# Graph layer: two norms from two products of one sum, bias addition on GpSimd, softmax links moved

## The chip, the cores and the metric

The kernel runs on one core of a Trainium2 chip. A core has five engines with instruction streams of their own: TensorE (PE, matrix products into PSUM), VectorE (DVE), ScalarE (ACT), GpSimd (POOL, here the issuer of indirect gathers) and SyncE (SP, here the issuer of plain transfers). They meet only at semaphores. The metric is the time of one execution on the device in microseconds (us); less is better.

## What is computed

Four graph layers over 50,000 nodes and 25,000 edges with 128 features, each followed by a residual sum and a layer norm. The change is in the third, a graph attention layer with an inner norm of its own:

```python
def _L2_gnn_ref(x, edge_index, edge_attr, W_l, b_l, W_r, b_r, W_e, att, bias, ln_w, ln_b):
    ...
    x_l = (x @ W_l + b_l).reshape(n, H, C)
    x_r = (x @ W_r + b_r).reshape(n, H, C)
    x_j = x_l[src]
    m = jax.nn.leaky_relu(x_j + x_r[tgt] + e_emb, NEG_SLOPE)
    logits = jnp.einsum('ehc,hc->eh', m, att)
    ...                                   # softmax over the edges of one target
    out = jax.ops.segment_sum(alpha[..., None] * x_j, tgt, num_segments=n)
    out = out.reshape(n, H * C) + bias
    out = jax.nn.gelu(out, approximate=False)
    h = out + x
    mu = jnp.mean(h, axis=-1, keepdims=True)
    var = jnp.mean((h - mu) ** 2, axis=-1, keepdims=True)
    return (h - mu) * jax.lax.rsqrt(var + LN_EPS) * ln_w + ln_b
...
x = _layernorm(x + _L2_gnn_ref(x, edge_index, edge_weight1, ...), axis=-1)
x = _layernorm(x + _L3_gnn_ref(x, src, dst, L3_gnn_W), axis=-1)
```

So a row x, which a norm has already centred, goes through two norms: norm 1 of gelu(...) + x, scaled by ln_w and shifted by ln_b, and norm 2 of that plus x.

## The kernel before

The edges are sorted by target and cut into 49 tiles of 512. The layer (`layer2`) is one loop of steps c = 0 to 62, written out for each engine by hand; the order of the statements is the order on the engine. In step c edge tile c gets its logits; tile e0 = c - 11 is weighed with the finished softmax and its plain nodes are projected; e1 = c - 12 goes through gelu and norm 1, e2 = c - 13 is scaled and centred again, e3 = c - 14 goes through norm 2 and is stored. Each tile has three blocks of 512 rows there: two of plain nodes (psP, two PSUM banks) and one of edge targets (psU, one bank). Up to step 48 all of this runs in every step; in steps 49 to 62 only the node part is left.

The softmax runs over seven runs s of seven tiles. Its serial part, the "links", is a chain of small VectorE operations on 112 or fewer columns: in step 7s+8 `running_maximum`, `maximum_between_chunks` and `exponents`, in step 7s+9 `running_sum`, `sum_between_chunks` and `weights`. PE turns columns to rows and back between them. I call such a step a softmax step and every other an ordinary one.

Norm 1 before, for tile e1 and then e2: PE multiplies the gelu (features on partitions) by the centring matrix I - 1/128, which also turns it to rows (L1363, psP and psU, operand `turns`); VectorE adds x (L1713, L1717: `pre1`); ScalarE squares it (L1538), VectorE sums (L1586), ScalarE forms rstd (L1564); VectorE scales (L1582: `n`); PE turns the three blocks back (L1358, from `n`); ScalarE applies ln_w and ln_b (L1528, L1532, into `turns`); PE centres and turns to rows a second time (L1363); VectorE adds x (L1748, L1765: `pre2`). Norm 2: square (L1569), sum (L1586), rstd (L1524), and scaling to x3o (L1582) and x4o (half on L1582, half in four ScalarE copies, L1543). `pre2` is a single buffer: VectorE may refill it only when x3o and x4o of the tile before are made.

The logits of tile c come from z, zsl and zl on VectorE (L1754, L1758, L1761). At the end of a step PE turns the gathered rows of edge tile c+1 (`turn_edges`, L1358 from `xd_xs`) and projects the nodes of e0 (L1471, `y`); the next step begins with L1391. POOL issues eight gathers for a tile (L1292), two tiles ahead, each time after PE has turned a tile. `by_row`, `quarters` and `scaled` only cut 1536 columns in 128-column rows and multiply each by its factor.

## Time and profile before

| | |
|---|---|
| runs | 3518.30, 3537.49, 3529.63 us (median 3529.63) |
| the profiled execution | 3540.14 us |
| span of its trace | 3538.4 us |
| mean granted clock of TensorE, share of full | 0.878 |
| PE busy, of the span | 2701.9 us (76%) |
| DVE | 2616.7 us (74%) |
| ACT | 2012.3 us (57%) |
| POOL | 1863.6 us (53%) |

The profile gives, for one execution, when each engine worked and what released it when it had waited. A row of a timeline has the start and the duration; the next row of the same engine often starts some 0.08 us before the printed end, since operations overlap a little. The difference of two starts is therefore what an operation costs its engine, and the duration is what another engine waits for. The third layer runs from about 1896 to 2955 us of the span: steps 0 to 10 end near 2050 us, the tail without edges begins near 2745 us. The fourth layer takes the rest, 583 us.

### The profile page before, as it was taken

Reading aid. Unit: us, or ns where it says so; the run is one execution under the profiler, and the core shown is the slowest. Engines: PE = TensorE matmul, PEld = TensorE weight load, DVE = VectorE, ACT = ScalarE, POOL = GpSimd, SP = SyncE. Lnnn points to the kernel's source line nnn. Section 1 sums busy time; section 2 is a strip of 40 time slices with the busy share of each in tenths; the row PEclk is TensorE's granted clock in tenths of the full one; section 3 lists DMA queues with packets and bytes.
Section 4 is the critical chain, followed back from the end, with each engine's and each line's share of the span. In section 5 each row is a group of like instructions: output and inputs, shape, how many; then the busy total and the mean of one; then the engine's idle time right before and its main releaser. Section 6 shows DMA issues by size and latency. Waiting matters only on the chain. (4 is left out here: it accounts for less than half of the span.)

```text
span 3538.4 us, 46258 instructions
## 1 busy us (share of the span) xinstructions
PE 2701.9 (76%) x14325; PEld 1792.3 (51%) x14325; DVE 2616.7 (74%) x3171; ACT 2012.3 (57%) x3400; POOL 1863.6 (53%) x1771
## 2 busy tenths in 40 slices
PE   7799999689999778878785789999999774332332
PEld 3466666466666545555553246666666553221221
DVE  6589999889999868888884269999999994222322
ACT  0167777556665558878784258888888782111111
POOL 4477787333333276766663654554453003666665
PEclk6699999899999989999997899999999996566655
DMA  6357666556666556666662156666666653222221
GB/s 202 100 173 222 212 221 220 189 176 197 197 202 199 160 167 207 210 207 208 197 205 74 47 159 172 188 196 193 183 194 174 183 171 107 58 64 63 74 69 39
DMA packets 474800, 573.34 MB, mean 162 GB/s; under 512 B 65347, under 2 KB 283133, under 8 KB 474431
## 3 DMA queue, kind: packets, MB, share of 16 engines
q1 hardware_dynamic: 412744, 457.19, 42.0%
q0 software_dynamic: 56480, 111.88, 11.6%
q8 instruction: 119, 1.95, 0.2%
q10 hardware_dynamic: 5334, 1.32, 0.2%
q14 instruction: 123, 1.00, 0.1%
HBM read 353.51 MB, written 220.55 MB: 162 GB/s over the span
## 5 line engine op out<-in xcount | busy, mean ns | idle before, releaser
L1292 POOL DMA_INDIRECT g_xd_xs<-table_x,dst_row x196 | 211.8, 1081 | 360.4 <-PE g_psT L1358 250.7
L1804 POOL DMA_INDIRECT f_xs<-table_x,src_row x196 | 192.0, 980 | 312.5 <-POOLq L1216 253.1
L775 POOL DMA_INDIRECT c_xs<-table_x,src_row x196 | 185.5, 946 | 303.9 <-PE c_psT L916 250.6
L765 POOL DMA_INDIRECT c_xs<-table_h,src_row x196 | 206.9, 1056 | 193.0 <-PE c_psT L909 94.0
L1867 ACT ACTIVATE f_reluT<-f_psY 128x512 f32<-128x512 f32 x49 | 29.3, 597 | 472.6 <-DMA table_x<-g_x3o 329.2
L497 POOL DMA_INDIRECT xs<-in_x,src_i x196 | 224.7, 1147 | 101.6 <-issue 54.0
L482 POOL DMA_INDIRECT xd<-in_x,dst_i x196 | 222.9, 1137 | 96.3 <-issue 47.9
L1811 POOL DMA_INDIRECT out<-f_xo,end_i x196 | 198.7, 1014 | 121.1 <-DVE f_xo L1904 61.6
L1292 POOL DMA_INDIRECT g_xd_xs<-table_x,src_row x196 | 218.6, 1116 | 59.8 <-issue 59.8
L765 POOL DMA_INDIRECT c_xd<-table_h,dst_row x196 | 200.8, 1025 | 59.8 <-issue 59.8
L1363 PE MATMUL g_psP<-w_center,g_turns 128*128 128x128 f32 x1568 | 197.1, 279 | 13.6 <-ACT g_turns L1492 9.1
L1363 PEld LDWEIGHTS g_psP<-w_center,g_turns 128*128 128x128 f32 x1568 | 187.0, 194 | 32.5 <-ACT g_turns L1492 12.7
L1586 DVE TENSOR_REDUCE g_var<-g_sq 128x12 f32<-128x1536 f32 x98 | 171.7, 1752 | 37.8 <-ACT g_sq L1538 34.6
L1841 PE MATMUL f_psE<-w_center,f_reluT 128*128 128x128 f32 x392 | 79.8, 368 | 153.2 <-ACT f_reluT L1867 117.7
L1896 DVE SCALAR_TENSOR_TENSOR f_pre<-f_x3r,f_psE 128x512 f32<-128x512 f32 x49 | 33.5, 684 | 203.8 <-DMA out<-g_x4o 193.1
L1023 ACT ACTIVATE c_xo<-c_pre,c_rstd 128x128 f32<-128x128 f32 x588 | 182.4, 390 | 1.6
L1841 PEld LDWEIGHTS f_psE<-w_center,f_reluT 128*128 128x128 f32 x392 | 70.5, 270 | 165.0 <-ACT f_reluT L1867 124.6
L1846 PE MATMUL f_psY<-f_red,w_w3t 128*128 128x512 f32 x98 | 77.6, 885 | 99.7 <-issue 68.6
L1122 DVE TENSOR_TENSOR c_pre<-c_psE,c_x1r 128x512 f32<-128x512 f32 x147 | 98.6, 686 | 73.0 <-remote 55.2
L1913 DVE TENSOR_TENSOR_SCAN f_red<-f_cont,f_red,f_psT 128x512 f32<-128x512 uint8 x48 | 61.3, 1277 | 112.7 <-DMA g_packed<-logits 76.0
L1471 PE MATMUL g_psP<-g_nodeT,w_w_l 128*128 128x512 f32 x196 | 107.1, 673 | 45.7 <-DVE g_pre L1748 44.2
L1853 PE MATMUL f_psT<-w_ident,f_xs 128*128 128x128 f32 x196 | 45.2, 374 | 116.9 <-DMA f_xs<-table_x,src_row 111.1
(330 smaller groups left out, 8669.8 us busy)
## 6 DMA issues: line engine op xcount, KB each, us to landing
g_share<-shares SPq DMA_DIRECT2D x196, 192.0 KB
xn<-in_x SPq DMA_DIRECT2D x49, 512.0 KB
table_x<-xo SPq DMA_DIRECT2D x49, 512.0 KB
table_x1b<-xb SPq DMA_DIRECT2D x49, 512.0 KB
c_xn<-table_x SPq DMA_DIRECT2D x49, 512.0 KB
table_h<-c_xo SPq DMA_DIRECT2D x49, 512.0 KB
c_xn<-table_h SPq DMA_DIRECT2D x49, 512.0 KB
c_x1r<-table_x1b SPq DMA_DIRECT2D x49, 512.0 KB
```

The costliest lines, as they stand in the source:

```text
L482: pool.indirect_dma_start(out=quarters(h.xd0[:, s, :])[j], out_offset=None, in_=io["x0"], in_offset=edge_index(h.dst_i, n, j)).then_inc(h. ...
L497: pool.indirect_dma_start(out=quarters(h.xs0[:, s, :])[j], out_offset=None, in_=io["x0"], in_offset=edge_index(h.src_i, n, j)).then_inc(h. ...
L765: pool.indirect_dma_start(out=quarters(rows[:, s, :])[j], out_offset=None, in_=table, in_offset=edge_index(columns, now.n, j)).then_inc(la ...
L775: pool.indirect_dma_start(out=quarters(xs[:, s, :])[j], out_offset=None, in_=table, in_offset=edge_index(h.src_row, now.n, j)).then_inc(sr ...
L1023: ins = nc.scalar.activation(quarters(xo[:, g.slot, j // 4, :])[j % 4], quarters(pre[:, g.slot, j // 4, :])[j % 4], ACT.Copy, scale=rstd[: ...
L1292: pool.indirect_dma_start(out=quarters(xd_xs[:, s, k, :])[j], out_offset=None, in_=table, in_offset=edge_index(columns, now.n, j)).then_in ...
L1363: ins = nc.tensor.matmul(o, x, h.w["center"][:, :], start=True, stop=True)
L1471: ins = nc.tensor.matmul(psP[:, k, :], h.w["w_l"][:, :], nodeT[:, e0 % 2, k, :], start=True, stop=True)
L1586: nc.vector.tensor_reduce(var[:, :], by_row(sq[:, :, :].rearrange("p b n -> p (b n)")), AX_X, ALU.add).then_inc(ready, 1)
L1804: pool.indirect_dma_start(out=quarters(xs[:, s, :])[j], out_offset=None, in_=table, in_offset=edge_index(h.src_row, now.n, j)).then_inc(sr ...
L1811: pool.indirect_dma_start(out=io["out"], out_offset=edge_index(h.end_i, old.n, j), in_=quarters(xo[:, s, :])[j], in_offset=None, bounds_ch ...
L1841: ins = nc.tensor.matmul(o, x, h.w["center"][:, :], start=True, stop=True)
```

## The change

Since x is centred already, centring gelu + x equals centring gelu and adding x. The new kernel adds x before the product, with features on partitions (`gx`), and takes two products of that one sum: with the centring matrix C, for the squares of norm 1, and with C diag(ln_w) C, called `twice_centred`, for what norm 2 needs. Dividing by the deviation of norm 1 is done behind the second product, and C ln_b, as a row (`ln_b_row`), is added to x by GpSimd.

For each node tile, removed: twelve PE transposes of `n`, two ScalarE operations with ln_w and ln_b, the VectorE scaling of `n`, the VectorE half of x4o. Added: four PE transposes of the edge rows (`xe_turned`), four more ScalarE copies for x4o (eight in all), one GpSimd addition over 128x1536. The four residual additions on VectorE become two additions into `gx` (1024 and 512 columns), two scalings from PSUM (`scaled_n`, `scaled_e`) and one addition over 1536 columns. The square of norm 1 is read from PSUM in two parts; the squares of the two norms get buffers of their own. Moved: the square of norm 2 to the next step's start on ScalarE, the z products on PE ahead of the softmax's row products, and on VectorE the links behind x3o and behind the scaling. In the set-up two VectorE scalings, two PE products and two VectorE copies are new. The core of the diff:

```diff
+            nc.vector.tensor_scalar(centre_w[:, :], h.w["center"][:, :], h.col("ln_w"), None, ALU.mult).then_inc(norm_rows, 1)
+            nc.vector.tensor_scalar(spread_b[:, :], ones[:, :], h.col("ln_b"), None, ALU.mult).then_inc(norm_rows, 1)
...
+            nc.tensor.matmul(psm[:, P:2 * P], h.w["center"][:, :], centre_w[:, :], start=True, stop=True)
+            nc.tensor.matmul(psm[:, 2 * P:3 * P], spread_b[:, :], h.w["center"][:, :],
+                             start=True, stop=True).then_inc(norm_turned, 1)
...
+            for n in range(ends):
+                if is_tile(n):
+                    gather(n)
+                e = n - 2 - lag
+                if is_tile(e):
+                    pool.wait_ge(n_turned, e + 1)
+                    pool.wait_ge(xe_turned, e + 1)
+                    wait(pool, x3_ready, e - 1)
+                    x = by_row(rows[:, e % 4, :, :].rearrange("p b n -> p (b n)"))
+                    nc.gpsimd.tensor_tensor(x, x, bias, ALU.add).then_inc(biased, 1)
...
@@ block.tensor
                 if is_tile(e1):
-                    pe.wait_ge(gn_ready, e1 + 1)
+                    pe.wait_ge(x2e_landed[e1 % 4], 16 * (e1 // 4 + 1))
+                    wait(pe, scaled_e, e1 - 1)
+                    turned_rows(psU[:, 0, :], rows[:, e1 % 4, 2, :]).then_inc(xe_turned, 1)
+                    pe.wait_ge(gxn_ready, e1 + 1)
                     for k in range(2):
-                        ins = centred(psP[:, k, :], gn[:, k, :])
+                        ins = to_rows(psP[:, k, :], gx[:, e1 % 2, k, :], h.w["center"])
                     ins.then_inc(en_ready, 1)
...
                 if is_tile(e2):
-                    pe.wait_ge(n1_ready, e2 + 1)
-                    pe.wait_ge(n_kept, min(e0 + 1, STEPS))
+                    pe.wait_ge(sq1n_ready, min(e1 + 1, STEPS))
+                    wait(pe, scaled_n, e2)
                     for k in range(2):
-                        ins = turned_rows(psT[:, k, :], n1[:, k, :])
-                    ins.then_inc(n1n_turned, 1)
+                        ins = to_rows(psP[:, k, :], gx[:, e2 % 2, k, :], h.twice_centred)
+                    ins.then_inc(fn_ready, 1)
...
                     pe.wait_ge(n_kept, e0 + 1)
-                    wait(pe, pre1n_ready, e1 + 1)
-                    wait(pe, pre2n_ready, e2 + 1)
+                    wait(pe, sq1n_ready, e1 + 1)
+                    wait(pe, scaled_n, e2 + 1)
...
@@ block.scalar
-                    nc.scalar.activation(sq1[:, :, :], pre1[:, :, :], ACT.Square).then_inc(sq1_ready, 1)
+                    act.wait_ge(en_ready, e1 + 1)
+                    wait(act, var1_ready, e1)
+                    nc.scalar.activation(sq1[:, 0:2, :], psP[:, :, :], ACT.Square).then_inc(sq1n_ready, 1)
+                    act.wait_ge(ee_ready, e1 + 1)
+                    nc.scalar.activation(sq1[:, 2, :], psU[:, 0, :], ACT.Square).then_inc(sq1e_ready, 1)
...
-                    for j in range(4):
-                        ins = nc.scalar.activation(quarters(x4o[:, 0, :])[j], quarters(pre2[:, 0, :])[j], ACT.Copy,
-                                                   scale=rstd2[:, j:j + 1])
-                    ins.then_inc(x4a_ready, 1)
+                    for k in range(2):
+                        for j in range(4):
+                            ins = nc.scalar.activation(quarters(x4o[:, k, :])[j], quarters(pre2[:, k, :])[j], ACT.Copy,
+                                                       scale=rstd2[:, 4 * k + j:4 * k + j + 1])
+                    ins.then_inc(x4_ready, 1)
...
@@ block.vector
+                if is_tile(e2):
+                    wait(dve, x3_ready, e2)
+                    wait(dve, x4_ready, e2)
+                    wait(dve, sq2_ready, e2)
+                    dve.wait_ge(rstd1_ready, e2 + 1)
+                    dve.wait_ge(fn_ready, e2 + 1)
+                    scaled(pre2[:, 0:2, :], psP[:, :, :], rstd1[:, e2 % 2, 0:8], 2, scaled_n)
...
+                    scaled(pre2[:, 2:3, :], psU[:, :, :], rstd1[:, e2 % 2, 8:12], 1, scaled_e)
+                    dve.wait_ge(biased, e2 + 1)
+                    dve.wait_ge(scaled_n, e2 + 1)
+                    dve.wait_ge(scaled_e, e2 + 1)
+                    nc.vector.tensor_tensor(pre2[:, :, :], pre2[:, :, :], rows[:, e2 % 4, :, :],
+                                            ALU.add).then_inc(pre2_ready, 1)
```

PE in an ordinary step, before: from the turning of the node rows (`xn`) to the first product of the next step.

```order
L1358 MATMUL g_psT<-w_ident,g_xn 128x128 x8
L1363 MATMUL g_psP<-w_center,g_turns 128x128 x8
L1363 MATMUL g_psU<-w_center,g_turns 128x128 x4
L1358 MATMUL g_psT<-w_ident,g_n 128x128 x8
L1358 MATMUL g_psU<-w_ident,g_n 128x128 x4
L1439 MATMUL g_psZ<-g_edgeT,w_w_r 128x512
L1440 MATMUL g_psZ<-g_erow,w_e_row 128x512
L1442 MATMUL g_psZ<-g_edgeT,w_lr 128x512
L1363 MATMUL g_psP<-w_center,g_turns 128x128 x8
L1363 MATMUL g_psU<-w_center,g_turns 128x128 x4
L1358 MATMUL g_psT<-w_ident,g_xd_xs 128x128 x8
L1471 MATMUL g_psP<-g_nodeT,w_w_l 128x512 x2
```

The same stretch of PE after the change (`rows` holds the node and edge rows).

```order
L1372 MATMUL g_psT<-w_ident,g_rows 128x128 x8
L1372 MATMUL g_psU<-w_ident,g_rows 128x128 x4
L1377 MATMUL g_psP<-w_center,g_gx 128x128 x8
L1377 MATMUL g_psU<-w_center,g_gx 128x128 x4
L1437 MATMUL g_psZ<-g_edgeT,w_w_r 128x512
L1438 MATMUL g_psZ<-g_erow,w_e_row 128x512
L1440 MATMUL g_psZ<-g_edgeT,w_lr 128x512
L1377 MATMUL g_psP<-twice_centred,g_gx 128x128 x8
L1377 MATMUL g_psU<-twice_centred,g_gx 128x128 x4
L1372 MATMUL g_psT<-w_ident,g_xd_xs 128x128 x8
L1479 MATMUL g_psP<-g_nodeT,w_w_l 128x512 x2
```

The transposes of `n` are gone, and the four of the edge rows stand ahead of the first product.

VectorE around x3o in step 7s+8, before (`m_row`, `m_in` and `m_line` are the link between chunks).

```order
L1713 TENSOR_TENSOR g_pre<-g_psP,g_xn 128x1024
L1717 TENSOR_TENSOR g_pre<-g_psU,g_x2e 128x512
L1604 COPY g_m_row<-g_psA 1x4x32
L1607 SCALAR_TENSOR_TENSOR g_m_in<-g_reach_row,g_m_row 1x132
L1609 COPY g_m_line<-g_m_in 1x128
L1611 COPY g_m_row<-g_m_in 1x4
L1582 TENSOR_TENSOR g_x3o<-g_pre,g_rstd 128x1536
L1582 TENSOR_TENSOR g_x4o<-g_pre,g_rstd 128x512
L1586 TENSOR_REDUCE g_var<-g_sq 128x12
```

VectorE there after the change.

```order
L1600 SCALAR_TENSOR_TENSOR g_m_here<-g_far,g_top 128x112
L1583 TENSOR_TENSOR g_x3o<-g_pre,g_rstd 128x1536
L1605 COPY g_m_row<-g_psA 1x4x32
L1608 SCALAR_TENSOR_TENSOR g_m_in<-g_reach_row,g_m_row 1x132
L1610 COPY g_m_line<-g_m_in 1x128
L1612 COPY g_m_row<-g_m_in 1x4
L1587 TENSOR_REDUCE g_var<-g_sq 128x12
L1583 TENSOR_TENSOR g_pre<-g_psP,g_rstd 128x1024
L1617 COPY g_m<-g_psA 128x1
```

The link now stands behind x3o, and the scaling from PSUM ahead of the exponents.

POOL after the change; before, only the gathers stand there.

```order
L1298 DMA g_xd_xs<-table_x,src_row 128x128 x4
L1311 TENSOR_TENSOR g_rows<-g_rows,ln_b_row 128x1536
L1298 DMA g_xd_xs<-table_x,dst_row 128x128 x4
```

The addition for a tile stands between the gathers of two edge tiles.

## Rows read from the trace of the kernel before

**Rows 1.** Windows: stretch, us, busy PE, PEld, DVE, ACT, POOL, clock, DMA share, GB/s.
```profile
2160.00:2745.00 585.00, 551.73 (x3043) 363.01 (x3042) 539.27 (x586) 487.13 (x707) 276.68 (x239) 1.00 0.67 189
```
**Rows 2.** DVE in one ordinary step, timeline (start, duration, what, idle before).
```profile
2463.11 1.76 DVE L1582 TENSOR_TENSOR g_x3o<-g_pre,g_rstd 128x1536 f32<-128x1536 f32 x1 [0.84 <-ACT g_rstd L1524]
2464.79 0.68 DVE L1582 TENSOR_TENSOR g_x4o<-g_pre,g_rstd 128x512 f32<-128x512 f32 x1
2466.25 1.75 DVE L1586 TENSOR_REDUCE g_var<-g_sq 128x12 f32<-128x1536 f32 x1 [0.77 <-ACT g_sq L1538]
2467.92 1.22 DVE L1748 TENSOR_TENSOR g_pre<-g_psP,g_xn 128x1024 f32<-128x1024 f32 x1
2469.05 0.68 DVE L1754 TENSOR_TENSOR g_z<-g_psZ,g_values 128x512 f32<-128x512 f32 x1
...
2470.31 0.68 DVE L1761 SCALAR_TENSOR_TENSOR g_zl<-g_z 128x512 f32<-128x512 f32 x1
...
2476.84 1.28 DVE L1705 TENSOR_TENSOR_SCAN g_agg<-g_share,g_agg,g_values 128x512 f32<-128x512 f32 x1
```
**Rows 3.** PE in the same step, timeline.
```profile
2469.28 1.96 PE L1471 MATMUL g_psP<-g_nodeT,w_w_l 128*128 128x512 f32 x4 [0.17 <-DVE g_pre L1748]
2471.09 1.10 PE L1391 MATMUL g_psZ<-g_edgeT,w_w_l 128*128 128x512 f32 x2
...
2472.97 1.05 PE L1402 MATMUL g_psA<-g_zl,g_att_a 128*36 128x512 f32 x2
...
2474.81 1.09 PE L1358 MATMUL g_psT<-w_ident,g_xn 128*128 128x128 f32 x8
2475.74 1.95 PE L1363 MATMUL g_psP<-w_center,g_turns 128*128 128x128 f32 x16
```
**Rows 4.** ACT in the same step, timeline.
```profile
2461.04 1.28 ACT L1512 ACT_TABLE_LOAD   x1
2462.33 0.30 ACT L1516 ACTIVATE g_lnv<-g_var,eps 128x8 f32<-128x8 f32 x1
...
2462.99 1.19 ACT L1528 ACTIVATE g_turns<-g_psT,cols 128x1024 f32<-128x1024 f32 x1
...
2466.11 1.27 ACT L1543 ACTIVATE g_x4o<-g_pre,g_rstd 128x128 f32<-128x128 f32 x4
2467.28 0.68 ACT L1549 ACTIVATE g_low<-g_psZ,x2b_self 128x512 f32<-128x512 f32 x1
...
2476.10 1.01 ACT L1501 ACTIVATE g_nodeT<-g_psT 128x1024 f32<-128x1024 f32 x1
2477.00 1.11 ACT L1505 ACTIVATE g_values<-g_psZ,cols 128x1024 f32<-128x1024 f32 x1
2478.00 0.59 ACT L1510 ACTIVATE g_alike<-g_psA 36x512 f32<-36x512 f32 x1
```
**Rows 5.** POOL in the same step, timeline.
```profile
2469.89 0.95 POOL L1292 DMA_INDIRECT g_xd_xs<-table_x,dst_row  x1 [6.07 <-PE g_psT L1358]
...
2479.18 0.94 POOL L1292 DMA_INDIRECT g_xd_xs<-table_x,src_row  x1 [0.30 <-issue]
```
**Rows 6.** POOL in the set-up, view of groups by line and form.
```profile
L419 POOL IOTA i_rev_row<- 98x256 int32 x1 | 0.3, 337 | 0.0
```
**Rows 7.** DVE, timeline: z in steps 7s+8 and 7s+9, and the link.
```profile
2504.18 0.68 DVE L1754 TENSOR_TENSOR g_z<-g_psZ,g_values 128x512 f32<-128x512 f32 x1
...
2515.94 0.28 DVE L1604 COPY g_m_row<-g_psA 1x128 f32<-1x128 f32 x1
...
2517.24 1.76 DVE L1582 TENSOR_TENSOR g_x3o<-g_pre,g_rstd 128x1536 f32<-128x1536 f32 x1 [0.23 <-DVE g_m_row L1611]
...
2544.80 0.68 DVE L1754 TENSOR_TENSOR g_z<-g_psZ,g_values 128x512 f32<-128x512 f32 x1
```
**Rows 8.** DVE in the tail, timeline.
```profile
2877.93 1.20 DVE L1713 TENSOR_TENSOR g_pre<-g_psP,g_xn 128x1024 f32<-128x1024 f32 x1
...
2892.60 1.20 DVE L1713 TENSOR_TENSOR g_pre<-g_psP,g_xn 128x1024 f32<-128x1024 f32 x1
```

More of the change, by code:

```diff
@@ L341, in _ @@
             link(nc.vector.tensor_scalar(h.x2b_self[:, :], h.b_self[:, :], 0.2, None, ALU.mult))
+            dve.wait_ge(norm_turned, 1)
+            link(nc.vector.tensor_copy(h.twice_centred[:, :], psm[:, P:2 * P]))
+            link(nc.vector.tensor_copy(h.ln_b_row[:, :], psm[:, 2 * P:3 * P]))
             dve.wait_ge(rows_turned, 1)
@@ L1229, in layer2 @@
         edgeT, nodeT = sb("edgeT", [P, 2, 2, TILE]), sb("nodeT", [P, 2, 2, TILE])
[L1230 removed]
+        rows = sb("rows", [P, 4, 3, TILE])
         erow = sb("erow", [P, 2, TILE])
@@ L1283, in _, with gather @@
         def _(pool):
-            def step(t):
-                now = t.tile(0)
-                s = now.slot
-                wait(pool, src_landed[s], 64 * now.half)
-                wait(pool, dst_landed[s], 64 * now.half)
-                wait(pool, e_turned, now.n - 1)
+            def gather(n):
+                s = n % 2
+                wait(pool, src_landed[s], 64 * (n // 2))
+                wait(pool, dst_landed[s], 64 * (n // 2))
+                wait(pool, e_turned, n - 1)
                 for k, columns, landed in ((0, h.dst_row, dst_landed), (1, h.src_row, src_landed)):
@@ L1452, in _ @@
                                      start=True, stop=True).then_inc(d_cols, 1)
-                if is_tile(e2):
-                    pe.wait_ge(affn_ready, e2 + 1)
-                    pe.wait_ge(pre1n_ready, min(e1 + 1, STEPS))
-                    for k in range(2):
-                        ins = centred(psP[:, k, :], affT[:, k, :])
-                    ins.then_inc(fn_ready, 1)
-                    pe.wait_ge(affe_ready, e2 + 1)
-                    centred(psU[:, 0, :], affT[:, 2, :]).then_inc(fe_ready, 1)
                 if is_tile(c + 1):
@@ L1463, in _ @@
                     wait(pe, n_kept, e0 + 1)
-                    wait(pe, affn_ready, e2 + 1)
                     turn_edges(c + 1)
@@ L1931, in build @@
         h.w_edge_row, h.w_e_row = square("w_edge_row"), square("w_e_row")
+        h.twice_centred, h.ln_b_row = square("twice_centred"), square("ln_b_row")
         h.b_vs = sb("b_vs", [P, 2])
```

183 lines of the change are left out of this document (75 added, 108 removed).

## The prediction

> **What bounds the kernel now.** I read the windows first, then one step of the third layer on each engine. In the full steps of that layer, 585 us of the trace, PE is busy 551.7 us, VectorE 539.3 and ScalarE 487.1, at a clock of 1.00 [rows 1]. No engine is the only bound; what counts is how the engines' orders close from one step to the next. The reader is to see a step of 17.56 us: z starts at 2469.05 and, two ordinary steps on, at 2504.18 [rows 2, 7]. VectorE works 15.95 us of it and waits twice, 0.84 us for the factor of norm 2 and 0.77 us for the square of norm 1 [rows 2]; both come from ScalarE, which runs without a pause through its chain from nodeT to the x4o copies [rows 4]. POOL idles 6 us of a step [rows 5]. So a gain needs three things together: PE's 94%, VectorE's 91% and the ScalarE chain all have to shrink.
>
> **PE.** Eight transposes take 0.93 us of PE (2474.81 to 2475.74), eight centring products 1.79 [rows 3], whose rows count two passes a product (x16 against x8). Twelve transposes go (1.4 us), four come (0.5 us): 0.9 us less; the products with `twice_centred` are as many and of the same form as the second centring. PE needs some 15.8 us.
>
> **VectorE.** The half of x4o goes: 0.65 us (0.68 long) [rows 2]. The rest only changes places: scaling `n` and four additions were 1.69 + 1.12 + 0.60 + 1.13 + 0.60 = 5.1 us; now gx 1.13 + 0.60, scalings from PSUM 1.13 + 0.60, the 1536 addition 1.67 and 0.1 for the wait on the scaling just before it: 5.2 us. An operation of a form costs the same from PSUM as from SBUF (pre2 over 1024 columns 1.22 us) [rows 2]. VectorE needs 15.4 us.
>
> **ScalarE.** The two affine operations go (1.19 us the one [rows 4]), four copies of x4o come: four take 1.17 us (2466.11 to 2467.28), eight 2.34, and the last one ends 0.10 later [rows 4]. The square of norm 1 is cut in two and reads PSUM. PSUM forms of 1024 columns cost 0.90 (nodeT, 2476.10 to 2477.00) to about 1.1 us (affine); I take 0.95, and 0.60 for the 512 part, from `low` (0.68 long) [rows 4]. Two table loads per step stay. ScalarE needs 14.9 us.
>
> **The loop that now sets the step.** `pre2` is still one buffer, and y still waits until VectorE has emptied psP. So the cycle is: y, L1391 and L1392, the logits' two products, turning the node rows; on ScalarE nodeT, values, alike, table load, two logarithms, exponential, the two squares, eight copies; on VectorE the scaling; back to y. In order: 1.81 (2469.28 to 2471.09) + 1.88 (to 2472.97) + 1.84 (to 2474.81) + 1.09 + 0.03 = 6.65 on PE [rows 3]; 0.90 + 1.00 + 0.60 + 1.29 + 0.66 (2462.33 to 2462.99) + 0.95 + 0.60 + 2.44 = 8.44 on ScalarE [rows 4]; 0.03 + 1.22 + 0.14 = 1.39 for the scaling and the way back to PE [rows 2, 3] (0.14 is from the end of pre2 at 2469.14 to y). Together 16.48 us, above all three sums of work, so it closes last; 1.08 less than 17.56. Bounds: with PE alone bounding 15.8, with the squares at the price of the affine pair 16.8.
>
> What is moved hardly counts: the z products stand earlier on PE by what the transposes took; the square of norm 2 moves over a gap of ScalarE; SP issues the node rows behind one wait instead of two, a step and more ahead of their use. The four transposes of edge rows wait for psU of the last but one tile, long free.
>
> **GpSimd's addition.** No row shows GpSimd adding tensors. From below I take VectorE's 1.76 us for the same columns [rows 2]; GpSimd's own index row, 256 columns in 0.34 us [rows 6], is 1.3 ns a column and would make it 2.0, my value. From above I take the slowest elementwise form of the trace, the scan with 1.28 us for 512 columns [rows 2], 3.8 us. The gate holds the addition until x3o of the step is done. Behind it are queued the eight gathers of a tile, 10.2 us from first to last [rows 5]. From the end of x3o to the turning of those rows I count a step and 2.2 us, 18.7 us; less 10.2 to 11.2 for gathers, some 2 for the last landing and 0.8 for starting leaves about 5 us for the addition. Up to there it is hidden. VectorE asks for the result behind both scalings, 5 us after x3o: also hidden. So at 2.0 as at 3.8 us the term is nothing. If the cover is gone, the excess over 5 us falls on VectorE in every step. The Trainium skill (GPSIMD Engine Reference, Performance versus the Vector engine) gives 4497 ns for such an addition over 2048 columns; an estimate from that page for 1536 would be 3.4 us, and the sum would stay.
>
> **The sum.** From step 11 the full steps that are ordinary and settled number 24: 24 x 1.08 = 25.9 us. Softmax steps: both together take 40.62 us now (z at 2504.18 and 2544.80) [rows 7]. VectorE is full there, so the links are 40.62 - 2 x 15.95 = 8.7 of it; afterwards it needs 2 x 15.4 + 8.7 = 39.5 and some 0.1 of waits: 1.0 less, five pairs, 5 us. Tail: a step is 14.67 us (2877.93 to 2892.60) [rows 8], all VectorE; afterwards 15.4 less z, zsl and zl (1.86) plus 0.2 of waits is 13.7; eight steps, 8 us. The set-up adds six small operations, at most 1 us. In all 25.9 + 5 + 8 - 1 = 38 us. On the profiled execution's 3540.1 that is 3502; that execution lies 10.5 us above the median of the runs, so I predict 3529.6 - 38 = 3492 us.
>
> **Rival 1: the addition holds up VectorE's small operations (about the same as before).** In a softmax step the link now starts right where the addition does, behind x3o. It is four operations, 1.30 us before (2515.94 to 2517.24) [rows 7], among them a scan of two SBUF rows and SBUF copies. If VectorE and GpSimd cannot read SBUF at once, the link waits for the rest of the addition, and the step with it, since VectorE is full there. Twelve softmax steps have an addition. At 1.76 us an addition (VectorE's own row) the price is 12 x 1.5 = 18 us, result 3510; at 3.8 us 12 x 3.5 = 42, result 3534. In ordinary steps the gate puts the addition beside the reduction, the scaling from PSUM, z and zsl; the first operation with two SBUF operands, zl, comes 4.6 us behind x3o. For it: VectorE is without a pause at exactly this place, so that any delay counts in full. Against it: gathers run on POOL through half of each step and no row of VectorE is longer for it; but a gather is no addition of tensors. The first two of the four operations may also be through before the addition starts, some 0.8 us behind its release; then the price is smaller. The Trainium skill states it as a rule (SBUF — State Buffer, Who interferes with whom): a VectorE instruction with two SBUF inputs and a GpSimd instruction that reads SBUF exclude each other for a whole instruction. With the 3.4 us of the page on GpSimd it would cost 37 us and leave 3529.
>
> **Rival 2: slower.** Same mechanism, decided by the length of the addition with its start. Beyond 4.6 us zl waits in every step, and in the tail the 1536 addition. At 5 us with 0.8 for starting: 12 x 4.7 = 56 for the links, and 32 ordinary and tail steps x 1.2 = 38; 3492 + 94 = 3586. It outweighs the gain from about 3.5 us of length on. Without any exclusion the same side is reached only when the addition is over 5 us and holds the gathers back: at 8 us the turning comes 3 us late in every second step, 24 x 1.5 = 36 and more.
>
> **Rival 3: the step does not close at 16.5.** If squares from PSUM cost 1.19 + 0.77 or x4o's copies 0.35 us each, ScalarE's chain grows by 0.3 to 0.5 us, and if z or the values then fall behind PE, a step gains 0.4 us and not 1.1: 3492 + 24 x 0.7 = 3509.
>
> **How the numbers follow.** About 0.5%, 18 us, is what a measurement can tell from no change here. Forecast 3492, chance 0.50, own range 3476 to 3511. Rival 1: 0.27, 3510 to 3534, a fifth of it on the side of faster. Rival 3: 0.10, at the border. Rival 2: 0.13. Faster: 0.48 + 0.05 + 0.04 = 0.57; same: 0.02 + 0.22 + 0.06 = 0.30; slower 0.13. The range leaves out rival 2 and a little below: 3474 to 3538.
>
> **What would show it.** In the trace after: ordinary steps from z to z of 16.5 us; ahead of the scaling (1024 columns) VectorE idle for about 0.5 us, released by x4o on ScalarE; x3o to the next reduction without idle time in ordinary steps. Rival 1 shows as idle time of 1 to 3.5 us in front of `m_in` or `m_line`, and only there; rival 2 as idle time in front of zl or the 1536 addition, or of PE in front of the turning of edges. POOL's new row gives the length that decides. Wrong at the root would be a step whose last wait is neither x4o nor GpSimd.

## The result: slower by 0.7%

| | before | after |
|---|---|---|
| median of 6 runs each, taken together | 3520.78 us (3518.30 to 3537.49) | 3550.61 us (3535.71 to 3561.02) |
| ratio after / before | | 1.0066, interval 1.0045 to 1.0088 |
| the profiled execution | 3540.14 us | 3549.30 us |
| its span | 3538.4 us | 3547.5 us |
| third layer, first z to last x3o | 1027.3 us | 1039.1 us |

The change makes the kernel slower by about 0.7%. The whole difference of the spans, 9 us, lies in the third layer, which is 11.8 us longer. The forecast was 3492, with a range up to 3538; the time lies outside it.

The window over the full steps, after (stretch, us, busy PE, PEld, DVE, ACT, POOL, clock, DMA share, GB/s), to be read against [rows 1]:

```profile
2160.00:2745.00 585.00, 532.14 (x2705) 334.42 (x2705) 532.62 (x539) 453.19 (x778) 413.08 (x271) 0.94 0.65 185
```

POOL went from 277 to 413 us. PE, VectorE and ScalarE are less busy than before, in part because the change gives them less to do in a step. But the steps did not get shorter by as much, and the clock of PE, 1.00 before, is 0.94. I then looked at the distance from z to z, step by step:

| | before | after | predicted |
|---|---|---|---|
| ordinary step | 17.56 | 16.40, some 17.3 to 17.5 | 16.48 |
| pair of softmax steps (mean of five) | 40.7 | 46.7 (22.9 + 23.8) | 39.6 |
| step behind the pair | 17.56 | 18.5 to 18.8 | 16.48 |
| tail, ordinary (x3o to x3o) | 14.66 to 14.92 | 13.56 | 13.7 |
| tail, last softmax step | 16.72 | 20.16 | not worked out by itself |

VectorE in an ordinary step, after (timeline: start, duration, what, idle before), against [rows 2]:

```profile
2465.89 1.27 DVE L1705 TENSOR_TENSOR_SCAN g_agg<-g_share,g_agg,g_values 128x512 f32<-128x512 f32 x1
2467.70 1.76 DVE L1583 TENSOR_TENSOR g_x3o<-g_pre,g_rstd 128x1536 f32<-128x1536 f32 x1 [0.54 <-issue]
2469.37 1.74 DVE L1587 TENSOR_REDUCE g_var<-g_sq 128x12 f32<-128x1536 f32 x1
2471.48 1.23 DVE L1583 TENSOR_TENSOR g_pre<-g_psP,g_rstd 128x1024 f32<-128x1024 f32 x1 [0.36 <-ACT g_x4o L1549]
...
2473.88 0.68 DVE L1754 SCALAR_TENSOR_TENSOR g_zl<-g_z 128x512 f32<-128x512 f32 x1
```

The scaling waits for x4o as foretold, 0.36 us. zl, two SBUF operands, is undisturbed at 0.68.

VectorE in a softmax step, where the link stands behind x3o, against [rows 7]; then POOL over the same time:

```profile
2518.13 1.73 DVE L1583 TENSOR_TENSOR g_x3o<-g_pre,g_rstd 128x1536 f32<-128x1536 f32 x1
2519.78 0.27 DVE L1605 COPY g_m_row<-g_psA 1x128 f32<-1x128 f32 x1
2520.09 4.34 DVE L1608 TENSOR_TENSOR_SCAN g_m_in<-g_reach_row,g_m_row 1x132 f32<-1x132 f32 x1
2524.46 0.21 DVE L1610 COPY g_m_line<-g_m_in 1x128 f32<-1x128 f32 x1
```

```profile
2518.37 2.31 POOL L1298 DMA_INDIRECT g_xd_xs<-table_x,src_row  x1 [0.30 <-issue]
2520.70 3.44 POOL L1311 TENSOR_TENSOR g_rows<-g_rows,ln_b_row 128x1536 f32<-128x1536 f32 x1
2524.29 0.96 POOL L1298 DMA_INDIRECT g_xd_xs<-table_x,dst_row  x1 [0.16 <-issue]
```

The scan over 132 elements of one partition, 0.42 us before, is printed with 4.34 us. It ends at 2524.43, the addition at 2524.14; in all twelve softmax steps that have an addition the link's scan ends 0.28 to 0.30 us behind the addition's end. `m_in` took 3.66 to 4.35 us in six of the seven softmax runs and 0.42 in the first, which has no addition beside it; `d_in`, the link of the second softmax step, 3.53 to 3.54 in six of seven. VectorE shows no idle time in front of it. What takes an operand from PSUM is not longer: of the layer's rows beside an addition (behind 2100 us), 35 scalings over 1024 columns, 35 reductions and 25 rows of z, none is more than 0.01 us above the median of its form. One thing stays open: in three of the twelve, this one among them, the scan's row begins 0.61 us before the addition's, and nothing here shows what holds it until then.

PE behind that link, against [rows 3], and one window over it after and then before:

```profile
2524.73 0.38 PE L1464 MATMUL g_psA<-g_ones,g_m_line 1*128 1x1 f32 x2 [2.17 <-DVE g_m_line L1610]
...
2527.82 3.75 PE L1479 MATMUL g_psP<-g_nodeT,w_w_l 128*128 128x512 f32 x4 [1.56 <-DVE g_pre L1583]
```

```profile
2524.00:2534.00 10.00, 7.71 (x19) 3.55 (x20) 9.66 (x17) 4.68 (x7) 8.01 (x8) 0.66 0.59 150
```

```profile
2524.00:2534.00 10.00, 9.30 (x44) 5.31 (x44) 9.86 (x13) 8.10 (x11) 7.82 (x8) 1.00 0.77 200
```

PE waits twice, 2.17 and 1.56 us, and then y takes 3.75 us instead of 1.96: at 1.2 instead of 2.4 GHz for most of it. The second wait alone is not new: in the same place of the kernel before PE waits 1.32 and 1.53 us in the two softmax steps, and y takes 1.96.

The last thing is where the 17.35 us steps come from. POOL after, against [rows 5], and PE at the end of that stretch:

```profile
2469.63 3.46 POOL L1311 TENSOR_TENSOR g_rows<-g_rows,ln_b_row 128x1536 f32<-128x1536 f32 x1 [1.71 <-DVE g_x3o L1583]
2473.23 0.96 POOL L1298 DMA_INDIRECT g_xd_xs<-table_x,dst_row  x1
...
2475.75 2.12 POOL L1298 DMA_INDIRECT g_xd_xs<-table_x,dst_row  x1 [0.30 <-issue]
...
2484.61 2.06 POOL L1298 DMA_INDIRECT g_xd_xs<-table_x,src_row  x1 [0.30 <-issue]
2486.68 3.45 POOL L1311 TENSOR_TENSOR g_rows<-g_rows,ln_b_row 128x1536 f32<-128x1536 f32 x1
```

```profile
2489.46 1.07 PE L1372 MATMUL g_psT<-w_ident,g_xd_xs 128*128 128x128 f32 x8 [1.16 <-DMA g_xd_xs<-table_x,src_row]
```

From addition to addition POOL needs 17.05 us without a pause, more than the step of 16.40. Here the gate has held it back first (1.71 us), the gathers start that much later, and PE waits 1.16 us for gathered rows. It is not so in every step: the next addition follows 16.70 us later, and 1.72 of them are again a wait for the gate.

Why is one gather 0.94 us long and another 2.12? In the kernel before, VectorE and then POOL:

```profile
2471.50 1.75 DVE L1582 TENSOR_TENSOR g_n<-g_pre,g_rstd 128x1536 f32<-128x1536 f32 x1
```

```profile
2472.39 1.68 POOL L1292 DMA_INDIRECT g_xd_xs<-table_x,dst_row  x1 [0.30 <-issue]
...
2480.43 0.95 POOL L1292 DMA_INDIRECT g_xd_xs<-table_x,src_row  x1 [0.31 <-issue]
```

The long gather begins while VectorE scales `n` from two SBUF operands, and ends (2474.07) 0.82 us behind that operation's end (2473.25). Between 2100 and 2700 us of that trace 95 of 261 gathers take more than 1.05 us, and every one of them ends 0.75 to 0.83 us behind the end of a VectorE operation with two SBUF operands; after the change it is 93 of 248, with 0.74 to 0.84. Those that begin beside a reduction or an operation with a PSUM operand take 0.94 to 0.97. So GpSimd is kept out by such operations, in the kernel before too; what of a gather it is that waits, no run separates. The last gather of the stretch above (2484.61) met x3o (2484.10 to 2485.86) and is 1.12 us longer for it, about what PE then waits.

### The profile page after: what moved, and what is told of

It is laid out like the page before. It is cut to its first block and busy times, and to the rows that moved or that the text cites. A ratio compares the mean times of both kernels' runs of the same rounds, so it can differ in the third digit from the quotient of the medians.

```text
span 3547.5 us, 45437 instructions
## 1 busy us (share of the span) xinstructions
PE 2671.1 (75%) x13937; PEld 1752.1 (49%) x13937; DVE 2631.8 (74%) x3126; ACT 1979.8 (56%) x3547; POOL 2065.8 (58%) x1820
## 3 DMA queue, kind: packets, MB, share of 16 engines
q10 hardware_dynamic: 5334, 1.32, 0.2%
q14 instruction: 123, 1.01, 0.1%
## 5 line engine op out<-in xcount | busy, mean ns | idle before, releaser
L1311 POOL TENSOR_TENSOR g_rows<-g_rows,ln_b_row 128x1536 f32<-128x1536 f32 x49 | 168.8, 3444 | 273.6 <-DVE g_x3o L1583 264.1
L1298 POOL DMA_INDIRECT g_xd_xs<-table_x,src_row x196 | 247.8, 1264 | 59.8 <-issue 59.8
L1479 PE MATMUL g_psP<-g_nodeT,w_w_l 128*128 128x512 f32 x196 | 117.8, 732 | 37.6 <-DVE g_pre L1583 36.8
L1080 ACT ACTIVATE c_xnT<-c_psT 128x512 f32<-128x512 f32 x196 | 110.9, 594 | 40.7 <-issue 36.2
L956 PE MATMUL c_psV<-c_xsT,w_v 128*128 128x512 f32 x196 | 109.9, 644 | 28.9 <-issue 16.3
```

What stands on the lines that cost most here:

```text
L1298: pool.indirect_dma_start(out=quarters(xd_xs[:, s, k, :])[j], out_offset=None, in_=table, in_offset=edge_index(columns, n, j)).then_inc(la ...
L1311: nc.gpsimd.tensor_tensor(x, x, bias, ALU.add).then_inc(biased, 1)
L1479: ins = nc.tensor.matmul(psP[:, k, :], h.w["w_l"][:, :], nodeT[:, e0 % 2, k, :], start=True, stop=True)
```

## The experiments

The first seven kernels are the changed one with one edit. The eighth has two edits, the ninth adds a condition and takes back the move of the links, and the tenth adds one edit to the ninth. They ran in three groups, each group on one chip beside the kernel before; the kernel before took 3530.16 us in the first, 3339.04 in the second and 3533.86 in the third. Between groups only ratios are compared. Where I give steps, they are from z to z.

### Without the addition

The row addition on GpSimd, its gates and VectorE's wait for it are left out; the output lacks the shift by ln_b.

```diff
-                e = n - 2 - lag
-                if is_tile(e):
-                    pool.wait_ge(n_turned, e + 1)
-                    pool.wait_ge(xe_turned, e + 1)
-                    wait(pool, x3_ready, e - 1)
-                    x = by_row(rows[:, e % 4, :, :].rearrange("p b n -> p (b n)"))
-                    nc.gpsimd.tensor_tensor(x, x, bias, ALU.add).then_inc(biased, 1)
...
-                    dve.wait_ge(biased, e2 + 1)
```

> The changed kernel without GpSimd's addition and without the waits on it; the shift by ln_b is left out of the result. Theory A (exclusion: while GpSimd adds, a VectorE operation with two SBUF operands waits for the whole addition, 3.44 us; and the addition delays the gathers queued behind it): the scan m_in takes 0.42 us again and not 4.34, the two softmax steps together some 39 to 40 us and not 46.8, every ordinary step 16.4 us and none 17.35; in all about 55 us less than the changed kernel, some 3490 to 3500. Theory B (the long scan is late for another reason, its input from PE or the clock, and the addition costs only GpSimd's queue): the pair stays above 45 us, only the 17.35 us steps go, 3535 to 3540.

Measured 3487.03 us, ratio 0.988 (0.9837 to 0.9923). Ordinary steps 16.40, pair 18.85 + 20.02 = 38.9, tail 13.54, `m_in` and `d_in` 0.42. The layer takes 974.2 us, 64.9 less than with the addition. So all of the loss, and of the missing gain, is the addition's doing. The rest of the change is worth 43 us by the medians (27 to 58 by the interval), where the sum said 38.

One step behind the second softmax step is still 18.05 us behind four of five complete pairs. PE there, and the window over it:

```profile
2518.36 1.61 PE L1398 MATMUL g_psZ<-g_edgeT,w_w_l 128*128 128x512 f32 x2 [2.29 <-DVE g_zl L1747]
2519.77 1.91 PE L1399 MATMUL g_psZ<-g_edgeT,w_w_l 128*128 128x512 f32 x2
```

```profile
2518.00:2524.00 6.00, 5.63 (x10) 1.65 (x11) 5.58 (x6) 2.04 (x2) 5.09 (x4) 0.72 0.72 169
```

PE had waited 2.29 us for zl, since `weights` stands ahead of it on VectorE, and then ran at a granted clock of 0.72; L1399 took 1.91 instead of 1.02 us, and VectorE waited 1.65 us for the edge rows. PE waits the same 2.29 us at this place in all five pairs, and in one of them L1399 takes 1.02 and the step 16.40; without the gate (below) it waits 2.29 us too and the steps behind are all 16.40. What decides whether the clock falls there is open.

### The links ahead of x3o again

```diff
-                if is_tile(e3):
-                    dve.wait_ge(rstd2_ready, e3 + 1)
-                    wait(dve, node_stored, 16 * e3)
-                    wait(dve, edge_stored, 16 * e3)
-                    scaled(x3o[:, :, :], pre2[:, :, :], rstd2[:, 8:20], 3, x3_ready)
                 s = run_at(c, runs + 1)
...
                     sum_between_chunks(s)
+                if is_tile(e3):
+                    dve.wait_ge(rstd2_ready, e3 + 1)
+                    wait(dve, node_stored, 16 * e3)
+                    wait(dve, edge_stored, 16 * e3)
+                    scaled(x3o[:, :, :], pre2[:, :, :], rstd2[:, 8:20], 3, x3_ready)
```

> The changed kernel with the links between chunks put back ahead of x3o on VectorE; nothing else. Theory A: the scans are 0.42 us, outside the addition; behind x3o stand reduction and scaling (2.8 us), then the exponents or weights, whose first operation with two SBUF operands now meets the addition's end and loses some 1.3 us. Pair 46.8 - 2 x 3.3 + 2 x 1.3 = 42.8 us, 12 steps, about 24 us less: 3525. Theory B: the pair does not get shorter, 3550.

Measured 3523.51 us, ratio 0.9986 (0.9959 to 1.0012). Both link scans are back at 0.42 us, so where the link stands relative to the addition decides. The pair falls only to 43.2 to 44.0, expected 42.8: VectorE now waits for the row from PE, 1.05 to 1.61 us. The first of the exponents with two SBUF operands takes 0.84 us instead of 0.34 beside the end of the addition. Some steps stay at 17.4, as PE still waits for gathers. In time this kernel can't be told from the kernel before.

```profile
2374.76 0.28 DVE L1605 COPY g_m_row<-g_psA 1x128 f32<-1x128 f32 x1 [1.51 <-PE g_psA L1388]
2375.07 0.42 DVE L1608 TENSOR_TENSOR_SCAN g_m_in<-g_reach_row,g_m_row 1x132 f32<-1x132 f32 x1
```

### Without the gate

```diff
-                    wait(pool, x3_ready, e - 1)
```

> The changed kernel without GpSimd's wait for x3o; the addition starts when PE has turned the edge rows. Theory A: it starts at about VectorE's gx addition; the scan for agg waits for it in every step, some 1.5 us, ordinary steps 17 to 18 us; the softmax link is free, pair near 41 to 43; the gathers are no longer late. In all between 3525 and 3560, and the scan for agg is the row that gets longer. Theory B: all ordinary steps 16.4 us, pair as before or shorter, 3530 or less, no row of VectorE longer.

Measured 3536.65 us, ratio 1.0015 (0.9993 to 1.0037). In the full steps most of the loss is gone: from step 15 on every ordinary step is 16.40, where 17 to 18 was expected, the step behind the pair too; a pair is 19.91 + 21.02 = 40.9. But now another operation of VectorE is held up in every step. POOL and then VectorE:

```profile
2467.34 3.45 POOL L1310 TENSOR_TENSOR g_rows<-g_rows,ln_b_row 128x1536 f32<-128x1536 f32 x1 [0.95 <-PE g_psU L1371]
```

```profile
2466.11 1.22 DVE L1691 TENSOR_TENSOR g_gx<-g_gx,g_nodeT 128x1024 f32<-128x1024 f32 x1
2467.30 0.69 DVE L1695 TENSOR_TENSOR g_gx<-g_gx,g_psU 128x512 f32<-128x512 f32 x1
2467.90 1.75 DVE L1586 TENSOR_REDUCE g_var<-g_sq 128x12 f32<-128x1536 f32 x1
2469.57 2.30 DVE L1704 TENSOR_TENSOR_SCAN g_agg<-g_share,g_agg,g_values 128x512 f32<-128x512 f32 x1
```

The addition starts at 2467.34, 0.15 us behind PE's turning of the edge rows (2467.19), as it does in all but a few steps of this kernel. Beside it VectorE runs an addition with a PSUM operand and a reduction of one buffer, both at their usual length (0.69, 1.75). Only the scan, from SBUF alone, lasts 2.30 us instead of 1.27. That 1.03 us falls in an ordinary step into the 0.9 us that VectorE of the changed kernel waits for ScalarE anyway (0.54 and 0.36). In the tail there is no such room and the addition meets a longer row: the addition of the values takes 3.87 instead of 0.69 us, a step 17.3 to 18.5 instead of 13.56, and that eats what the full steps win.

```profile
2824.21 3.87 DVE L1687 TENSOR_TENSOR g_values<-g_values 128x512 f32<-128x512 f32 x1
```

GpSimd's addition can be the one that waits. Early in the tail it starts while VectorE adds 1536 columns from two SBUF buffers, until 2770.22, and takes 4.25 us instead of 3.44:

```profile
2768.46 1.76 DVE L1761 TENSOR_TENSOR g_pre<-g_pre,g_rows 128x1536 f32<-128x1536 f32 x1
```

```profile
2769.25 4.25 POOL L1310 TENSOR_TENSOR g_rows<-g_rows,ln_b_row 128x1536 f32<-128x1536 f32 x1 [17.05 <-PE g_psU L1371]
```

### GpSimd writes and does not read

The addition is replaced by twelve fills of 128x128, in buffers that are no longer used; the shift by ln_b is left out.

```diff
-                    x = by_row(rows[:, e % 4, :, :].rearrange("p b n -> p (b n)"))
-                    nc.gpsimd.tensor_tensor(x, x, bias, ALU.add).then_inc(biased, 1)
+                    wait(pool, biased, 12 * e)
+                    for name in ['q0', 'k0', 'v0', 's0', 'q1', 'k1', 'v1', 's1', 'w_src', 'w_dst', 'w_node', 'w_red']:
+                        nc.gpsimd.memset(h.w[name][:, :], 0.0).then_inc(biased, 1)
```

> The changed kernel with the addition replaced by twelve memsets of 128x128 into buffers of earlier layers, under the same waits: GpSimd writes and reads nothing from SBUF; the shift by ln_b is left out. Tells whether it is reading that excludes (the rule of the Trainium skill, SBUF - State Buffer, Who interferes with whom). If so: m_in 0.42 us, pair 39 to 41 us, time near the run without addition if the memsets are no longer than 3.4 us. If any GpSimd work on SBUF excludes: m_in stays long by what is left of the memsets.

Measured 3493.35 us, ratio 0.989 (0.9847 to 0.9934), pair 39.1. `m_in` and `d_in` are 0.42 us. The second of them lies in the middle of the fills, which run from 2518.47 to 2520.38:

```profile
2518.47 0.21 POOL L1312 MEMSET w_q<- 128x128 f32 x1 [5.57 <-DVE g_x3o L1584]
```

```profile
2518.67 0.42 DVE L1640 TENSOR_TENSOR_SCAN g_d_in<-g_d_row 1x132 f32<-1x132 f32 x1
2519.13 0.35 DVE L1642 COPY g_d_line<-g_d_in 1x128 f32<-1x128 f32 x1
```

So this scan is not held up by GpSimd being busy with SBUF as such; its 0.42 us leaves no room even for one fill of 0.2 us. The SBUF copies behind it are a little longer beside the fills (0.35 here, 0.21 elsewhere; at most 0.14 more). A single long write was not tried, and a fill differs from the addition in more than reading, so that it is the reading that excludes is supported and not proved.

### The gate in the tail only

```diff
-                    wait(pool, x3_ready, e - 1)
+                    if not is_tile(e + 1 + lag):
+                        wait(pool, x3_ready, e - 1)
```

> The changed kernel with GpSimd's wait for x3o kept only in the steps without edges (the tail) and dropped in the full steps. Theory A (exclusion for the length of the addition, and gathers behind it): full steps as without any gate, 16.4 us ordinary and 40.9 us a pair, only the scan for agg longer by 1.0 us; tail 13.6 us a step, since there the addition lies beside the reduction and the scalings from PSUM. In all 3537 less 9 tail steps x 4.2 us = 3497 to 3502 us, faster than the kernel before by 0.8 to 1%. A theory in which the missing gate costs something elsewhere (the next layer, the transfers) gives more than 3510.

Measured 3313.34 us, ratio 0.9929 (0.9915 to 0.9942). Full steps as without the gate (16.40, pair 40.9), tail as with it (13.56), the tail's two link scans still 3.65 and 3.52. The gain is a little below the expected 0.8 to 1%. One line makes the changed kernel 0.7% faster than the kernel before.

### Half of the addition

Columns 0 to 767 alone are shifted.

```diff
-                    x = by_row(rows[:, e % 4, :, :].rearrange("p b n -> p (b n)"))
-                    nc.gpsimd.tensor_tensor(x, x, bias, ALU.add).then_inc(biased, 1)
+                    x = by_row(rows[:, e % 4, :, :].rearrange("p b n -> p (b n)"))[:, 0:6, :]
+                    nc.gpsimd.tensor_tensor(x, x, bias[:, 0:6, :], ALU.add).then_inc(biased, 1)
```

> The changed kernel with GpSimd's addition over 768 of the 1536 columns (the shift by ln_b is left out of the other half). Size test. Theory A: the addition takes 1.8 us, the scan m_in about 0.42 + 1.7 to 2.6 us instead of 4.34, d_in about 1.9 instead of 3.54; pair 43.2 us; the steps of 17.35 go. 3515 us. If the scan waits for something of its own, its time stays near 4.3.

One run, 3318.19 us, so its time has no interval. The addition takes 1.82 us, `m_in` 2.04 to 2.05 and `d_in` 1.86 to 1.91, the pair 42.0 (expected 43.2):

```profile
2380.31 2.04 DVE L1608 TENSOR_TENSOR_SCAN g_m_in<-g_reach_row,g_m_row 1x132 f32<-1x132 f32 x1
...
2525.12 1.86 DVE L1639 TENSOR_TENSOR_SCAN g_d_in<-g_d_row 1x132 f32<-1x132 f32 x1
```

The link's length follows the addition's. All ordinary steps are 16.40, but for the step behind the pair, 18.05 in three of five: with 1.6 us less on POOL, PE no longer waits for gathers.

### The addition on VectorE

```diff
+                    x = by_row(rows[:, e2 % 4, :, :].rearrange("p b n -> p (b n)"))
+                    nc.vector.tensor_tensor(x, x, h.ln_b_row[:, :].rearrange("p (o f) -> p o f", o=1)
+                                            .to_broadcast([P, 12, P]), ALU.add).then_inc(biased, 1)
                     dve.wait_ge(biased, e2 + 1)
```

> The changed kernel with the addition of the ln_b row moved from GpSimd to VectorE, just ahead of the 1536 addition. VectorE needs 15.4 + 1.7 = 17.1 us a step and nothing else: ordinary steps 17.1 us, pair 42.3, tail 15.2. In all 3487 + 24 x 0.7 + 6 x 3.4 + 9 x 1.7 = 3539 us. If VectorE hides the addition in its idle 1 us of a step, 3515.

Measured 3373.58 us, ratio 1.01 (1.0085 to 1.0116), worse than expected: ordinary steps 17.73 instead of 17.1, tail 16.87 instead of 15.2; the pair is 42.1, expected 42.3. The addition itself costs VectorE 1.79 us (2699.44 to 2701.23 below). In the tail a step grew by 3.3, from 13.56. VectorE (first) makes PE (second) wait for `gx`, and PE is then slow:

```profile
2699.44 1.75 DVE L1753 TENSOR_TENSOR g_rows<-g_rows,ln_b_row 128x1536 f32<-128x1536 f32 x1
2701.23 1.76 DVE L1758 TENSOR_TENSOR g_pre<-g_pre,g_rows 128x1536 f32<-128x1536 f32 x1
```

```profile
2706.03 3.78 PE L1370 MATMUL g_psP<-w_center,g_gx 128*128 128x128 f32 x16 [3.70 <-DVE g_gx L1685]
2709.61 1.85 PE L1370 MATMUL g_psU<-w_center,g_gx 128*128 128x128 f32 x8
```

The centring products, 2.05 us elsewhere, take 3.78 behind a wait of 3.70, and what ScalarE makes of them comes that much later. In the tail of this kernel the granted clock is 0.80 (2690 to 2760 us), in that of the changed one 0.96 (2800 to 2880). In full steps VectorE waits for PE in front of the scaling, 0.73 us in an ordinary step. That the clock makes up all of what the tail loses beyond 1.79 us is argued from these rows; no run holds the clock still.

### Two halves, links ahead

Columns 0 to 767 are shifted ahead of the four gathers by target, once the `gx` addition over 1024 columns is done; the rest ahead of the four gathers by source, behind x3o. The links stand ahead of x3o.

```diff
+                        if half == 0:
+                            pool.wait_ge(n_turned, e + 1)
+                            pool.wait_ge(xe_turned, e + 1)
+                            pool.wait_ge(gxn_ready, e + 1)
+                        else:
+                            wait(pool, x3_ready, e - 1)
+                        x = by_row(rows[:, e % 4, :, :].rearrange("p b n -> p (b n)"))[:, 6 * half:6 * half + 6, :]
+                        nc.gpsimd.tensor_tensor(x, x, bias, ALU.add).then_inc(biased, 1)
```

> The changed kernel with the addition cut in two halves of 768 columns: the first behind VectorE's gx addition (beside the gx addition from PSUM and the reduction), then the gathers of the target rows, the second half behind x3o (beside a reduction and the scaling from PSUM), then the gathers of the source rows; links between chunks ahead of x3o. Theory A: no VectorE operation gets longer, ordinary steps 16.4, pair 38.9 to 39.5, tail 13.6: 3487 to 3493 us, as without any addition. If a second start of the addition or late source gathers cost something, the ordinary steps show it: 16.4 to 17, up to 3505.

Measured 3322.41 us, ratio 0.995 (0.9936 to 0.9963), where the expected times come to 0.988 to 0.989. Ordinary steps are 16.40 as expected, the pair 42.2 to 42.9 and not 38.9 to 39.5: the copy of the row waits 1.47 us for PE in the first softmax step and 1.57 in the second, as with the links ahead above. The move of the links behind x3o, to which I had given no term, is thus worth some 1.5 us in each.

```profile
2381.36 0.28 DVE L1612 COPY g_m_row<-g_psA 1x128 f32<-1x128 f32 x1 [1.47 <-PE g_psA L1395]
```

### Two halves, links behind x3o, the second half behind the link

Against the run before:

```diff
                             wait(pool, x3_ready, e - 1)
+                            r = run_at(n - 1, runs + 1)
+                            if r is not None:
+                                pool.wait_ge(m_lined, r + 1)
+                            r = run_at(n - 1, runs + 2)
+                            if r is not None:
+                                pool.wait_ge(d_lined, r + 1)
```

> As the run with two halves, but the links stand behind x3o again (as in the changed kernel), and in softmax steps the second half waits for the link's last row to PE instead of x3o. Theory A (an addition of 1.8 us is free wherever 2.3 us of VectorE work with at most one SBUF operand lie beside it; links ahead of x3o cost 1.5 us each, the wait for their row from PE): no VectorE row longer, no wait before the link, pair 38.9 to 39.3 us, ordinary 16.4, tail 13.6 with softmax steps too. Ratio to the kernel before 0.988 to 0.990. If the pair stays above 40.5, something else than exclusion and the wait for PE costs in the softmax steps.

Measured 3490.85 us (6 runs), ratio 0.9883 (0.986 to 0.9906): the whole computation, at the ratio of the kernel without the addition (0.988). Ordinary steps 16.40, pair 18.94 + 20.04 for three of the five and 40.7 and 39.8 for the other two, `m_in` and `d_in` 0.42; the step behind the pair is 18.05 to 18.09 in four of five, as without the addition. It beats the kernel before by 1.2% and, by the two ratios, the changed one by 1.8%. POOL in an ordinary step:

```profile
2463.28 1.82 POOL L1322 TENSOR_TENSOR g_rows<-g_rows,ln_b_row 128x768 f32<-128x768 f32 x1 [1.10 <-DVE g_gx L1705]
...
2471.01 1.83 POOL L1322 TENSOR_TENSOR g_rows<-g_rows,ln_b_row 128x768 f32<-128x768 f32 x1
```

The first half runs beside VectorE's `gx` addition from PSUM and the reduction (2463.08 to 2465.44), the second beside the scaling from PSUM and ends (2472.84) before zl starts (2473.34). VectorE again waits 0.36 us for x4o in front of the scaling.

### The same, x4o shared out again

Two of the eight x4o copies go from ScalarE to VectorE, ahead of x3o.

```diff
+                    nc.vector.tensor_tensor(by_row(x4o[:, 1, 2 * P:4 * P]), by_row(pre2[:, 1, 2 * P:4 * P]),
+                                            rstd2[:, 6:8].rearrange("p (b o) -> p b o", o=1).to_broadcast([P, 2, P]),
+                                            ALU.mult).then_inc(x4v_ready, 1)
...
+                    for k, j in ((0, 0), (0, 1), (0, 2), (0, 3), (1, 0), (1, 1)):
+                        ins = nc.scalar.activation(quarters(x4o[:, k, :])[j], quarters(pre2[:, k, :])[j], ACT.Copy,
+                                                   scale=rstd2[:, 4 * k + j:4 * k + j + 1])
```

> The run before this one, with two of the eight copies for x4o moved from ScalarE to one VectorE operation of 256 columns. Tests whether the ordinary step is closed by the cycle through ScalarE's copies, as the prediction had it: ScalarE's chain gets 0.58 us shorter, VectorE's work 0.35 us longer; ordinary step 16.0 to 16.3 instead of 16.4, then closed by PE and VectorE; pairs 0.6 us longer, since VectorE is full there. About the same total. If the step stays at 16.40 or grows by 0.35, VectorE and not the copies closed it.

Measured 3502.29 us, ratio 0.991 (0.9881 to 0.9939): no gain, and 11 us more than the run before. Ordinary steps are 16.28 or 17.35. The 16.28 fits that the copies closed the step of 16.40, as predicted, and that the next bound lies only 0.12 us below. VectorE no longer waits for x4o, z comes earlier, and zl runs into the second half of the addition, which ends at 2467.50; zl ends at 2468.05:

```profile
2465.68 1.82 POOL L1322 TENSOR_TENSOR g_rows<-g_rows,ln_b_row 128x768 f32<-128x768 f32 x1
```

```profile
2466.30 1.75 DVE L1773 SCALAR_TENSOR_TENSOR g_zl<-g_z 128x512 f32<-128x512 f32 x1
```

## Why the prediction was wrong

**What held.** PE, VectorE, ScalarE and the cycle over y: ordinary steps are 16.40 us, predicted 16.48, and the wait that closes last is the scaling's for x4o, as named (0.36 us, foretold about 0.5). The tail is 13.56, predicted 13.7. Softmax steps without the addition take 38.9 a pair, predicted 39.6. Without the addition the kernel took 3487 us where the sum said 3492. The total agrees in part because small errors cancel: from trace to trace a pair gives 1.8 us and not 1.0, and the step behind it, 18.05 in four of five, loses 0.5 where 1.08 was counted as won; why PE's clock falls there is open.

**The step that failed** is "So at 2.0 as at 3.8 us the term is nothing". The runs showed 65 us of the layer in its place. It failed in two ways, the link and POOL's queue, and its length was off as well.

1. *The link.* The cover was checked for ordinary steps (zl, 4.6 us behind x3o) and for POOL's queue, but in softmax steps the link stands where x3o ends, and there is no cover at all. I had that as rival 1 with 0.27. It is now the case shown: the link lasts as long as the addition (3.44 us: 3.5 to 4.35; 1.82 us: 1.9 to 2.05; moved away: 0.42). Twelve links at 3.1 to 3.9 more each are some 40 us; rival 1 gave 42 at its upper end.
2. *POOL's queue.* "10.2 us from first to last" is misread: [rows 5] ends with the seventh of the eight gathers. The eighth ends at 2481.38 (2480.43 + 0.95), 11.5 us behind the first start. And the gathers did not stay as they were: the eight of a tile take 11.0 to 13.7 us after the change, 13.4 in the stretch shown (2473.23 to 2486.67), since they now stand beside other VectorE operations (a gather takes 1.27 us on average between 2100 and 2700 us, 1.16 before). With 13.4 the count that gave "about 5 us for the addition" gives 2.5, less than the 3.44 measured. It costs 0.9 to 1.1 us in nine ordinary steps.
3. *The length.* I took 2.0 us from the index row [rows 6], an operation of one written buffer, for one that reads two; it is 3.44. The estimate from the Trainium skill (GPSIMD Engine Reference, Performance versus the Vector engine), 3.4 us, was the better one, and the trace agrees. The length alone did not decide: 3.44 lies inside the 2.0 to 3.8 for which I had put the term at nothing.

**Rival 1 and its bounds.** Its price was capped at the links, with "only there" for its trace. The runs show two things behind it: the late link makes PE wait 2.17 and 1.56 us and the clock then falls to 0.66, so y takes 3.75 us instead of 1.96 and the product behind it 1.69 instead of 1.10; and the step behind the pair is 18.5 to 18.8 us, where it is at most 18.1 without the addition. Of the 64.9 us that the addition costs, 39 lie in the five complete pairs of the full steps (46.7 less 38.9 each; their ten links alone make 34), 5 in the steps behind them, 9 in the 17.35 us steps, 4 in the last step before the tail, and 5 in the tail behind it. The other 3 lie in the first steps. Rival 1 at 3534 was right in kind and 17 us short; both it and the forecast stood on a time before of 3529.6, and the six runs gave 3520.8, so against those it was 25 short.

**Exclusion.** The Trainium skill (SBUF — State Buffer, Who interferes with whom) states that a VectorE instruction with two SBUF inputs and a GpSimd instruction reading SBUF exclude each other for a whole instruction. The runs agree with it, in size and in both directions: for scans, two-operand additions and zl on VectorE, and for the addition of 4.25 us on GpSimd. With a PSUM operand and in the reduction VectorE was not held up, and beside the short writes neither. I had it before me and gave it 0.27. What I set against it was that no row of VectorE is longer beside a gather. That is so, to within some 0.06 us (0.42 and 0.68 us rows beside gathers), but I looked at one side only: in the same trace POOL's gathers are up to 1 us longer beside VectorE operations with two SBUF operands, as shown above. The trace of before held evidence for the exclusion, and I took it for evidence against.

**How it was to show.** I said "idle time of 1 to 3.5 us in front of `m_in`". It shows as the printed duration of `m_in`; VectorE has no idle time there.

**Rival 2** (zl in every step) did not come true with the gate as written: the addition starts 0.2 us behind x3o's end and its end is 0.8 us before zl. Its kind appeared where something was moved: the tail without the gate (3.87 us), and zl at 1.75 us when x4o was shared out.

## What to carry to other kernels

Before an elementwise operation goes to GpSimd, list what VectorE runs from its start to its end: operations with two inputs from SBUF wait for it; those with an operand in PSUM and reductions did not. Fit it in beside these, cut in pieces if no gap is long enough, and let the semaphore of the small operation on the critical path release it (here 1.2% gained, where the addition in one piece right behind x3o cost 0.7%). Look for an exclusion on both engines: rows of one form that differ in length, on GpSimd as on VectorE. And count a queue to its last entry, with lengths that may grow when its neighbours move.

## What the hardware showed that I had not expected

- A VectorE instruction that GpSimd keeps out prints the wait as its own duration (0.42 becomes 4.34 us), with idle time 0. Such a row is found by comparing lengths of one form, not by looking for waits.
- GpSimd is kept out in the same way. All 95 long gathers of the kernel before end 0.75 to 0.83 us behind the end of a VectorE operation with two SBUF operands (1.68 instead of 0.94 us, for example). In the run without the gate an addition that starts during VectorE's takes 4.25 us instead of 3.44.
- The GpSimd addition costs 3.44 us for 1536 columns and 1.82 for 768; VectorE does the 1536 in 1.8.
- A gather on POOL takes 0.94 us or up to 2.31, with 0.30 between; the eight of a tile take 11.0 to 13.7 us after the change.
- PE's granted clock was 0.66 and 0.72 over windows of 10 and 6 us behind idle times of 2.17 and 1.56 us together and of 2.29 us alone, and single products then took nearly twice as long. The same 2.29 us of idle time did it in four of five softmax runs of one kernel and in none of another, and 1.53 us did not do it in the kernel before. So a late operation of VectorE can cost more than its own length (the tail with the addition on VectorE: 3.3 us for 1.79).
